# Attention and routed experts on one core: the opening of the pipeline rebuilt, two groups of heads of batch 0 laid out on chip, and filler matmuls on TensorE

## What is computed

```python
q = (x @ Wq).reshape(B, T, 16, 8).transpose(0, 2, 1, 3)       # x: layernorm of the input
k = (x @ Wk).reshape(B, T, 16, 8).transpose(0, 2, 1, 3)
v = (x @ Wv).reshape(B, T, 16, 64).transpose(0, 2, 1, 3)
scores = einsum('bhqd,bhkd->bhqk', q, k) / sqrt(8)            # causal mask, softmax
out = einsum('bhqk,bhkd->bhqd', softmax(scores), v) ... @ Wo  # added to the input
# then: layernorm, a gate over 8 experts, each expert takes its 64 best tokens of a batch,
# gelu(xin @ w1) @ w2, scaled by the gate's probability and added back
```

## Time and profile before

| What | Value |
|---|---|
| Median of 3 runs | 535.07 us (534.59 to 536.13) |
| The profiled execution, its own time | 537.27 us |
| Its span (first to last instruction) | 535.5 us |
| TensorE busy (PE) | 511.6 us, 96% |
| Weight loads (PEld) | 424.9 us, 79% |
| DVE, ACT, POOL busy | 79%, 74%, 49% |
| Mean granted TensorE clock | 0.996 |
| DMA | 45.71 MB, mean 85 GB/s |

### The profile page before, as it was taken

How to read it: one execution, slowest core, us unless ns; L and a number is a source line. 1 busy time by engine, 2 the same in 40 slices (tenths; PEclk the granted TensorE clock), 3 DMA queues, 4 the chain that set the end, 5 groups by cost and what they waited for, 6 DMA issues and landing times.

```text
span 535.5 us, 13983 instructions
## 1 busy us (share of the span) xinstructions
PE 511.6 (96%) x4783; PEld 424.9 (79%) x4783; DVE 423.9 (79%) x1081; ACT 398.1 (74%) x1379; POOL 264.3 (49%) x252
## 2 busy tenths in 40 slices
PE   2679999999999999999999999999999999999996
PEld 2458778788787787787787887877789999999996
DVE  6868889889888988889999999999974587644444
ACT  4788998989889898988989989899753643434330
...
DMA packets 49447, 45.71 MB, mean 85 GB/s; under 512 B 4208, under 2 KB 46192, under 8 KB 49392
## 3 DMA queue, kind: packets, MB, share of 16 engines
...
q10 hardware_dynamic: 1088, 0.85, 0.6%
...
## 4 chain that ended last, share of the span: by engine, by line
PE 87%; DVE 5%; DMA 3%; issue 2%; ACT 2%; SPq 1%; POOLq 0%; POOL 0%; ACTq 0%; DVEq 0%
PE ctx_ps L1266 16%; PE t_ps L1353 10%; PE misc_ps L1275 10%; PE t_ps L1239 5%; PE t_ps L1240 5%; PE t_ps L1249 5%; PE misc_ps L1177 4%; PE s_ps L1337 4%; PE misc_ps L1179 3%; PE misc_ps L1178 3%; PE s_ps L1225 3%; PE s_ps L1338 3%; PE s_ps L1339 3%; PE s_ps L1212 3%; PE s_ps L1221 2%
## 5 line engine op out<-in xcount | busy, mean ns | idle before, releaser
L580 ACT ACTIVATE prob<-s_ps,neg_max 128x128 f32<-128x128 f32 (+1 forms) x512 | 210.6, 443 | 1.0 <-DVE neg_max L1051 0.7
L504 POOL TENSOR_TENSOR probn<-prob,inv 128x1024 f32<-128x1024 f32 x64 | 121.2, 1894 | 37.5 <-DVE inv L1072 37.4
L580 ACT ACTIVATION_READ_ACCUMULATOR prob<-s_ps,neg_max 128x1 f32 x512 | 117.7, 230 | 0.0
L497 POOL TENSOR_TENSOR probn<-prob,inv 128x512 f32<-128x512 f32 x64 | 66.6, 1041 | 69.9 <-PE t_ps L1249 68.9
L628 ACT ACTIVATE hT<-s_ps 128x512 f32<-128x512 f32 x64 | 38.1, 598 | 64.3 <-PE s_ps L1339 61.7
L1008 DVE TENSOR_REDUCE neg_max<-s_ps 128x4 f32<-128x1024 f32 x63 | 76.4, 1212 | 3.5 <-PE s_ps L1225 1.3
L533 POOL TENSOR_TENSOR y_parts<-y_sb,y_parts 128x512 fp32r<-128x512 f32 x16 | 21.2, 1326 | 106.9 <-ACT y_parts L638 106.9
L1275 PE MATMUL misc_ps<-wo_sb,ctxT 128*128 128x128 f32 x512 | 67.8, 275 | 0.7 <-DVE x_all L827 0.7
L1275 PEld LDWEIGHTS misc_ps<-wo_sb,ctxT 128*128 128x128 f32 x512 | 62.2, 192 | 1.1 <-issue 1.1
L1239 PE MATMUL t_ps<-ident,probn 128*128 128x128 f32 x256 | 61.7, 281 | 0.0
L1240 PE MATMUL t_ps<-ident,probn 128*128 128x128 f32 x256 | 60.1, 275 | 0.0
...
## 6 DMA issues: line engine op xcount, KB each, us to landing
...
```

The source lines that it names most:

```text
L497: nc.gpsimd.tensor_tensor(probn[r][:, 0:HG * P].rearrange("p (i k) -> p i k", i=HG), prob[r][:, 0:HG * P].rearrange("p (i k) -> p i k", i=HG),
L504: nc.gpsimd.tensor_tensor(probn[r][:, HG * P:].rearrange("p (i k) -> p i k", i=HG), prob[r][:, HG * P:].rearrange("p (i k) -> p i k", i=HG ...
L580: last = nc.scalar.activation(prob[r][:, first + i * keys:first + (i + 1) * keys], scores[:, i, :], ACT.Exp, bias=neg_max[:, r, block_, i: ...
```

## The change

It touches only what comes before or in the first steps of the pipeline. TensorE multiplies the identity by itself eight times before its first work and again at four later places (`keep_busy`), into PSUM banks that are free there. Groups 0 and 1 of batch 0 (`OWN = 2`) get their layout on chip: the repeated weights have 256 columns instead of 128 for queries and for keys, the product is made group by group (`first_own_product`, ahead of `queries_keys(0)`, and `second_own_product`), and the work after it is spread over DVE (`split_own`, `own_rows`), ACT (`split_own_keys`, `own_keys`) and POOL (`own_keys`). Groups 2 and 3 still come from DRAM, with all five loads and the low key stores on SP's queue. There are two sets of rows in DRAM, and the stores of batch b wait for the loads of batch b-2. `Wk` is loaded by SP second, `Wv` fourth. The low part of the value weights moves from DVE to POOL in two halves; the norm of batch 1 moves from DVE to POOL; copies for the mask operands move from POOL to DVE; zeroing is distributed anew. On TensorE, `queries_keys(1)` moves behind `first_scores(1, 0)`, the values of units 0 and 1 move ahead of the norms of batch 1, and the wait for the rows of batch 0 moves into step 0. The core of the diff, dedented:

```diff
-q_rows = nc.dram_tensor("q_rows", [H, 4, DK, T], F32).ap()
-k_rows = nc.dram_tensor("k_rows", [H, 4, DK, T], F32).ap()
+q_rows = [nc.dram_tensor(f"q_rows{r}", [H, 4, DK, T], F32).ap() for r in range(RING)]
+k_rows = [nc.dram_tensor(f"k_rows{r}", [H, 4, DK, T], F32).ap() for r in range(RING)]
...
-own_w_hi, own_w_lo = [k_diag[1][:, 0, k, :].rearrange("p (w c) -> p w c", w=2) for k in range(2)]
-own_hi = k_diag[1][:, 0, 2:4, :]
-own_ps = misc_ps[1][:, :].rearrange("p (w t) -> p w t", w=2)
+own_w_hi, own_w_lo = k_diag[1][:, 0, 0:2, :], k_diag[1][:, 0, 2:4, :]
+own_hi = [k_diag[1][:, 1, 2 * g:2 * g + 2, :] for g in range(OWN)]
+own_ps = [[misc_ps[1][:, 0:T], t_ps[0][:, 0:T]], [ctx_ps[:, 0, :], ctx_ps[:, 1, :]]]
...
     load_x(0)
+    sp.dma_start(wqk_raw[:, 1, :], w_k).then_inc(wqk_loaded[1], 16)
+    load_x(1)
     sp.dma_start(wv_raw[:, :], w_v).then_inc(wv_loaded, 16)
-    load_x(1)
     sp.dma_start(wo_sb[:, :, :], w_o.rearrange("(c p) n -> p c n", p=P)).then_inc(wo_loaded, 16)
     sp.dma_start(gate_sb[:, :], gate_w).then_inc(wo_loaded, 16)
     for b in range(B):
         sp.wait_ge(qk_hi_done, b + 1)
-        await_count(sp, qk_loaded, QK_LOADS * b)
-        store_rows(sp, qk_hi, Q_HI)
+        await_count(sp, qk_loaded, QK_LOADS * (b - 1))
+        store_rows(sp, b, qk_hi, Q_HI)
         if b > 0:
-            store_rows(sp, qk_hi, K_HI)
+            store_rows(sp, b, qk_hi, K_HI)
         sp.wait_ge(qk_lo_done, b + 1)
-        store_rows(sp, qk_lo, Q_LO)
-        if b > 0:
-            store_rows(sp, qk_lo, K_LO)
+        store_rows(sp, b, qk_lo, Q_LO)
+        store_rows(sp, b, qk_lo, K_LO)
         sp.wait_ge(qk_stored, QK_STORES * (b + 1))
         if b < RING:
-            sp.wait_ge(zeroed[b], 3 + b)
+            sp.wait_ge(zeroed[b], (G - OWN, G)[b])
         await_count(sp, s1_done, G * (b - 1))
-        if b == 0:
-            load_rows(b, slice(1, G), qk_loaded, range(2))
-        else:
-            load_rows(b, slice(0, G), qk_loaded)
+        load_rows(b, slice(OWN if b == 0 else 0, G), qk_loaded)
...
-        for rows, a in ((lower, 0), (upper, 1)):
-            nc.gpsimd.tensor_copy(half_masks[rows, 0, :], causal_halves[rows, a, :])
-            nc.gpsimd.tensor_copy(half_masks[rows, 1, :], causal_halves[rows, a, :])
-        nc.gpsimd.tensor_copy(half_rows[lower, 0, :], ident_bf[lower, :])
-        nc.gpsimd.tensor_copy(half_rows[upper, 0, :], low_rows_of[upper, 0, :])
-        nc.gpsimd.tensor_copy(half_rows[lower, 1, :], low_rows_of[lower, 1, :])
-        nc.gpsimd.tensor_copy(half_rows[upper, 1, :], ident_bf[upper, :]).then_inc(halves, 1)
-        pool.wait_ge(halves, 4)
+        pool.wait_ge(halves_copied, 2)
...
+    def second_norm():
+        pool.wait_ge(rstd1_done, 1)
+        pool.wait_ge(stats1, 2)
+        nc.gpsimd.tensor_tensor(var2[:, :], mv2[:, :, 1], eps_sb[:, :], ALU.add).then_inc(var1_done, 1)
+        pool.wait_ge(var1_done, 2)
+        nc.gpsimd.tensor_tensor(rstd2[:, :], var2[:, :], neg_half[:, :], ALU.pow).then_inc(rstd1_done, 1)
+        pool.wait_ge(rstd1_done, 2)
+        pool.wait_ge(xT_done, 1)
+        for tb in range(TB):
+            last = nc.gpsimd.tensor_scalar(xn1[:, tb, :], x_all[:, TB + tb, :], mv2[:, tb, 0:1], rstd2[:, tb:tb + 1],
+                                           ALU.subtract, ALU.mult)
+        last.then_inc(xn1_ready, 1)
+    def own_keys():
+        pool.wait_ge(own_k_done, 2)
+        pool.wait_ge(zeroed_own, OWN)
+        pool.wait_ge(wv_lo_done, 2)
+        for i in range(2, HG):
+            rows = slice(i * ROWS, (i + 1) * ROWS)
+            nc.gpsimd.tensor_copy(k_diag[0][rows, 1, i, :], f32(own_hi[1][rows, 1, :])).then_inc(own_keys_ready, 1)
+            pool.wait_ge(own_keys_ready, i)
+    def split_values_weights(k):
+        half = slice(k * 512, (k + 1) * 512)
+        pool.wait_ge(wv_hi_done, 1)
+        nc.gpsimd.tensor_tensor(wv_lo[:, half], wv_raw[:, half], f32(wv_hi[:, half]), ALU.subtract).then_inc(wv_lo_done, 1)
+    def zero_keys(r, j):
+        nc.gpsimd.tensor_scalar(k_diag[r][:, j, :, :].rearrange("p i t -> p (i t)"),
+                                eps_sb[:, 0:1].broadcast_to([P, HG * T]), 0.0, None, ALU.mult).then_inc(zeroed[r], 1)
...
     def batch(b, par):
         for j in range(G):
             u, r = b * G + j, j % RING
-            if j == 1 and has(b + 2, B):
+            if j == 1 and has(b + 2, B) and not at(u, (1,)):
                 norm1_scale(b + 2)
+            if at(u, (1,)):
+                zero_keys(1, 1)
             if j == 0 and has(b - 2, B):
                 norm_scale(b - 2)
...
+            if at(u, (1,)):
+                norm1_scale(2)
...
+            if at(u, (6,)):
+                numbers()
...
     mask_shapes()
-    norm1_scale(0)
-    pool.wait_ge(rstd1_done, 1)
+    first_scale()
+    zero_keys(1, 3)
     half_products()
-    norm1_scale(1)
-    for j in range(1, G):
-        nc.gpsimd.tensor_scalar(k_diag[1][:, j, :, :].rearrange("p i t -> p (i t)"),
-                                eps_sb[:, 0:1].broadcast_to([P, HG * T]), 0.0, None, ALU.mult).then_inc(zeroed[1], 1)
-    nc.gpsimd.iota(tok_no[:, :], pattern=[[P, TB]], base=0, channel_multiplier=1,
-                   allow_small_or_imprecise_dtypes=True).then_inc(numbered, 1)
-    nc.gpsimd.iota(col_no[:, :], pattern=[[1, T]], base=0, channel_multiplier=0,
-                   allow_small_or_imprecise_dtypes=True).then_inc(numbered, 1)
+    split_values_weights(0)
+    second_norm()
+    split_values_weights(1)
+    own_keys()
     batches(pool, batch)
...
+    def split_own_keys():
+        act.wait_ge(own_done, 2)
+        act.wait_ge(signs, 3)
+        nc.scalar.activation(own_hi[0][:, 1, :], own_ps[0][1], ACT.Copy, scale=hi_sign[:, 1:2]).then_inc(own_k_hi_done, 1)
+    def own_keys():
+        act.wait_ge(own_k_done, 1)
+        act.wait_ge(zeroed_own, OWN)
+        for i in range(2, HG):
+            rows = slice(i * ROWS, (i + 1) * ROWS)
+            last = nc.scalar.activation(k_diag[0][rows, 0, i, :], f32(own_hi[0][rows, 1, :]), ACT.Copy)
+        last.then_inc(own_keys_ready, 1)
...
-    split_norms(0, 0)
-    zero_keys(0, 0, zeroed_own)
+    split_norms(0, 0, t_ps[1])
     act.wait_ge(wv_loaded, 16)
-    nc.scalar.activation(wv_hi[:, :], wv_raw[:, :], ACT.Copy).then_inc(w_hi, 1)
+    nc.scalar.activation(wv_hi[:, :], wv_raw[:, :], ACT.Copy).then_inc(wv_hi_done, 1)
+    split_own_keys()
     split_qk(0)
+    own_keys()
     act.wait_ge(qk_hi_done, 1)
-    store_rows(act, qk_hi, K_HI)
-    act.wait_ge(qk_lo_done, 1)
-    store_rows(act, qk_lo, K_LO)
-    zero_keys(0, 3, zeroed[0])
-    split_norms(1, 1, misc_ps[1])
+    store_rows(act, 0, qk_hi, K_HI)
+    zero_keys(1, 2, zeroed[1])
     act.wait_ge(max0, 1)
     exps(0, 0, s0_ps, P, 0, exp0)
-    act.wait_ge(qk_stored, QK_STORES)
-    act.wait_ge(zeroed[0], 3)
-    for i in range(2, HG):
-        act.dma_start(f32(k_diag[0][i * ROWS:(i + 1) * ROWS, 1:G, i, :]),
-                      k_rows.rearrange("(j i) r d t -> i (r d) j t", j=G)[i][:, 1:G, :]).then_inc(qk_loaded, 16)
-    copy_values(0, 0, 0)
+    split_norms(1, 1, t_ps[1])
     act.wait_ge(max1, 1)
     exps(0, 1, s1_ps, T, HG * P, exp1)
+    copy_values(0, 0, 0, misc_ps[1])
+    copy_values(1, 1, 0, t_ps[0])
     split_qk(1)
-    copy_values(1, 1, 0, misc_ps[1])
     batches(act, batch)
     copy_turned(63, 1)
...
-    def split_own():
-        dve.wait_ge(own_done, 1)
+    def split_own(g):
+        dve.wait_ge(own_done, 2 * g + 1)
         dve.wait_ge(signs, 3)
-        for w in range(2):
-            nc.vector.tensor_scalar(own_hi[:, w, :], own_ps[:, w, :], hi_sign[:, w:w + 1], None,
-                                    ALU.mult).then_inc(own_hi_done, 1)
-        dve.wait_ge(own_hi_done, 2)
-        dve.wait_ge(zeroed_own, 1)
-        nc.vector.scalar_tensor_tensor(out=qT[0][:, 0, :], in0=own_ps[:, 0, :], scalar=is_low[:, 0:1],
-                                       in1=f32(own_hi[:, 0, :]), op0=ALU.mult, op1=ALU.add)
-        for i in range(HG):
+        nc.vector.tensor_scalar(own_hi[g][:, 0, :], own_ps[g][0], hi_sign[:, 0:1], None, ALU.mult).then_inc(own_q_hi_done, 1)
+        if g > 0:
+            dve.wait_ge(own_done, 2 * g + 2)
+            nc.vector.tensor_scalar(own_hi[g][:, 1, :], own_ps[g][1], hi_sign[:, 1:2], None,
+                                    ALU.mult).then_inc(own_k_hi_done, 1)
+    def own_rows(g):
+        dve.wait_ge(own_k_hi_done, g + 1)
+        nc.vector.scalar_tensor_tensor(out=own_hi[g][:, 1, :], in0=own_ps[g][1], scalar=is_low[:, 1:2],
+                                       in1=f32(own_hi[g][:, 1, :]), op0=ALU.mult, op1=ALU.add).then_inc(own_k_done, 1)
+        dve.wait_ge(own_q_hi_done, g + 1)
+        nc.vector.scalar_tensor_tensor(out=qT[0][:, g, :], in0=own_ps[g][0], scalar=is_low[:, 0:1],
+                                       in1=f32(own_hi[g][:, 0, :]), op0=ALU.mult, op1=ALU.add)
+        dve.wait_ge(own_k_done, g + 1)
+        dve.wait_ge(zeroed_own, OWN)
+        for i in range(2):
```

(98 more changed lines are left out.)

86 lines of the change are left out of this document (61 added, 25 removed).

## The result

The kernel became slower: **537.91 us** (median of 14 runs, 536.4 to 539.51) against 535.2 us (534.52 to 538.24, 14 runs) for the kernel before on the same chip, a ratio of 1.0042 with an interval of 1.0028 to 1.0055. The forecast was 533.1 with a range to 534.9.

The account below looks back on a forecast made before the run. Bound: the DMA chain of batch 1's rows before unit 4. Stores at 20.0 instead of 22.1, less 0.2, gave 2.0 us: 537.27 to 535.3, and with the median 2.2 below the profiled execution 533.1 us, range 530.9 to 534.9.

Parts of the forecast that it names:

- What bounds the kernel: TensorE's pace bounds it behind 37.5 us; before that, unit 4's first scores wait 2.5 us for batch 1's key loads.
- The size of the path before: From batch 1's first store to the need of its rows, 37.5 - 22.1 = 15.4 us in the kernel before.
- From the first store ... the change leaves that stretch alone: Batch 1's stores and loads up to unit 4 keep their 15.4 us; only 0.2 is lost for qk_lo.
- The first product: Opening on TensorE: starts at about 8.0, done at 9.3 or 8.7 instead of 11.05; gain 1.8 to 2.4.
- The norm's hindrance: Opening on DVE: POOL's zeroing beside the norm slows it by 0 to 0.4 us; taken as 0.3.
- Batch 1's stores at 20.0: SP begins storing batch 1's queries and keys at 20.0 instead of 22.1, decided by DVE's queue, added up to 18.3.
- POOL's list: POOL's work in the opening (value weights, norm, copies) ends at about 16, before DVE's rows at 17.7.
- POOL becomes the bound: Rival, 10%: TensorE waits for POOL's keys of group 1, delaying batch 1's stores; slower, 537 us.
- The filler: Extra matmuls in TensorE's waits lift the clock on the chain to batch 1's stores; worth 0.5 us, no cost counted.
- the second bound: Upper limit of the filler's worth: full clock for 12 matmuls on the chain, 1.3 us; the lower was 0.
- off again in the opening: Rival, 25%: no clock lift and DVE/POOL hindrance, or clock falls behind unit 4's wait (1.5 lost); gain 0 to 1.2, 534.5.
- the 10% case: The slower rival, 10%: POOL becomes the bound, if its work after 5.6 us takes 15.7 instead of 10.4; 537 us.

Follow-up runs that it names:

- the version with loops and six more matmuls: Changed kernel with both zeroings on ACT, qk_lo early, filler in loops, plus six more filler matmuls in the wait before unit 4; 534.57 us.
- the version with loops: Changed kernel with zeroing of batch 1's groups 0 and 3 on ACT, its qk_lo before step 0, filler in loops; 533.92 us, on another chip 534.08.
- the second profile of before: The kernel before, unchanged, profiled once more; that execution took 535.07 us.
- twenty tiny matmuls: The kernel before with 20 matmuls of 64 columns added in TensorE's first wait, into a free bank; 536.73 us, ratio 1.0039.

## Why the prediction was wrong, step by step

**What bounds the kernel: right.** Unit 4's first scores are released by the DMA in every profile but one (the version with loops and six more matmuls), 60 to 80 us is dense (20.00 of 20.00), and the time follows unit 4, except where the clock adds to it.

**The size of the path before: wrong by the execution.** The step read 15.4 us from the first store to the need out of one profile. A usual execution has 14.4 (21.89 to 36.28). Only the difference entered the sum, but the shorter wait hid a danger: before, TensorE stands 0.4 us before unit 4 and its clock holds; after, 2.2 to 2.4 us, and it seems to fall in most executions. The length of the wait alone does not decide it: the clock held after 2.5 us in the first profile of before and after 2.17 in that of after, and fell after 1.57 in the first profile of the version with loops.

**"From the first store ... the change leaves that stretch alone": the step that failed first.** In after it is 15.9 long. Inside it lies `qk_lo` of batch 1, which the change puts behind a zeroing of 2.15, a maximum of 1.21 and the refill; I charged 0.2 and measured a gap of 0.9. Moving `qk_lo` back closed what was left of it without filler (third pair from 24.09 to 23.80). And the last store lands 1.2 later (3.61 instead of the usual 2.4) where the packet on q8, TensorE's code as I read it, falls beside it.

**The first product: start mis-sized, end nearly right.** Forecast start 8.0 and end 8.7 to 9.3; measured 8.72 and about 9.5. The norm's hindrance, priced at 0.3, is 0.73, and the repeated weights, which I did not think of as hindered, lose 0.83 more. The first scores, forecast at 11.0, came at 13.23. The two key copies take 1.44, not 0.98 at most, beside POOL's half of the value weights, and end at 12.55. And TensorE itself is not free before 13.2, which the forecast did not ask: twelve more matmuls of 256 columns, 0.21 apart, and two of filler stand between the first product and the first scores, and from 8.72 on there is no gap. I had written that all filler lies in waits; the pair at 12.13 takes 0.9 and does not. Without any filler the first scores come at 13.33, so what the clock gave here the filler took back. This did not delay batch 1, whose chain runs over DVE's statistics.

I wrote that by the rule of the Trainium skill ("SBUF — State Buffer", on the shared port pair) a whole zeroing of 2.9 us would be added to one DVE step and the gain would be gone, and set it aside for 0.4 to 0.45 us a step. The size of a step was right and the number of steps wrong: one zeroing of 2.79 cost DVE 1.56, spread over four instructions, 0.39 each, and 1.1 us of the kernel's time, and I had charged 0.3 for the norm alone. The rule taken strictly does not come out of this trace: the norm began at 5.49, just behind the zeroing's start at 5.45, and ended at 6.82, before the zeroing did at 8.24.

**Batch 1's stores at 20.0: wrong by 1.75.** DVE's rows for the second group end at 18.5, where I had 17.7. And POOL's list, which I had at 16, ends at 19.2: 0.7 lost. POOL's timeline of after:

```profile
5.45 2.79 POOL L507 TENSOR_SCALAR k_diag_odd<-eps_sb 128x1024 fp32r<-128x1024 f32 x1
...
15.21 1.59 POOL L485 TENSOR_SCALAR xn<-x_all,mv,rstd 128x128 f32<-128x128 f32 x2
16.77 1.27 POOL L503 TENSOR_TENSOR wv_lo<-wv_raw,wv_hi 128x512 fp32r<-128x512 f32 x1
18.21 1.00 POOL L496 CAST k_diag_even<-k_diag_odd 32x256 fp32r<-32x256 f32 x2 [0.16 <-POOL wv_lo L503]
```

It waits until 14.1 for DVE's statistics of batch 1, which stand behind group 0's rows and `qk_lo`; then it needs 5.1 us in a row. `first_scores(1, 0)` follows at 19.30 and only at 20.12 `queries_keys(1)`, which is queued behind it and then waits for its norms' low part: 0.9 that the sum did not hold. The chain that ended last shows where that low part was:

```profile
17.97 1.58 ACT prob L642 x7
...
19.75 0.31 DVE xT_lo L901
```

I added DVE's queue up to 18.3 without a wait in it. In the trace its reciprocal waits 1.09 for ACT's exponentials of unit 0, which stand behind the turned norms and so behind POOL's norm. The low part of the norms, queued behind that reciprocal, is done at 20.06. The product and ACT's `qk_hi` take the rest as reckoned. So the rival "POOL becomes the bound" came true in part: POOL's keys of group 1 held `first_scores(1, 0)` back, from 17.7 on as said, but its list reached 19.2, not 21.3, and the wait between DVE and ACT decided the last 0.3.

**The filler: wrong in sign.** It lifts the clock as the second bound allowed and brings the stores 0.75 forward. It costs 2.0 to 2.2 in all. Of the two parts of the rival "off again in the opening", the second, a fall of the clock to 0.50 behind unit 4's wait, priced at 1.5, came true with 1.05 to 1.35; it was made an alternative to the first part, though both happened. That the time came out near the 537 of the 10% case is chance: that case had it from POOL's list alone. Two slips changed little: 22.1 less 20.0, less 0.2, is 1.9 and not 2.0, and the filler matmuls are 26.

**What stays open.** Of the filler's price, 0.9 is at unit 4. The profiles show a coincidence that holds for nearly all of them. With filler written out, the packet on q8 stands at 25.7 to 27.8 (six profiles) and the last store lands 3.48 to 3.74 after its issue; with loops at 27.9 to 30.4 and without filler at 35.9 to 39.7, and it lands after 2.34 to 2.75. The one exception is the second profile of before, 3.09 with no such packet near. TensorE's filler alone was changed from after to the kernels with loops or without filler, and this packet moved (26.98, 30.44, 36.37) while that of the other instruction queue did not (27.58, 28.24, 28.30): so the filler does move it, and it is TensorE's code. That the packet makes the landing late is argued from this, not shown: no run moved it and nothing else. Nor is it shown why its place differs by 7 us between the two profiles of before, or what makes up the rest of the 1.8 us that twenty tiny matmuls cost.
